# A gated convolution and mixture-of-experts layer on one Trainium2 core: small broadcast loads replaced by TensorE products, one load held back, one weight split moved two slots

## The chip, the cores and the metric

The kernel runs on one core of a Trainium2 chip. The metric is the device time of one execution in microseconds (us). Three executions of the kernel before gave 218.25, 219.16 and 421.25 us; their median is 219.16 us.

## The reference, cut to what matters

`x` and `ctx` are (16, 128, 256) in float32. The layer is

```python
x = x + tanh(g_xattn[0]) * xattn(ctx, ctx, layernorm(x), ssm_kernel, D)
x = x + tanh(g_ffn[0]) * ffn(layernorm(x), Wg, W1, W3, W2, sw1, sw3, sw2)
```

`xattn` splits the 128 channels into 16 heads of 8. For each head it forms the 8 x 8 products of the context with itself at every position, convolves each of them causally along the 256 positions with the head's filter `ssm_kernel[h]`, adds `D[h]` times the unconvolved product (the skip factor), multiplies with the normalised `x` and sums over one of the two channel indices. Adding `D[h]` to the filter's first tap gives the same result, since that tap multiplies the product at its own position.

`ffn` is a mixture of 8 experts (hidden size 352, top 1 of a softmax, 256 tokens of room per expert) plus one shared expert that sees every token: `silu(x W1) * (x W3) @ W2`, times the gate.

## The kernel before, in words

The work runs in *slots*, a loop over `s` that every engine writes out in its own program, and the engines meet at semaphores. The 16 batches form 4 groups of 4. Slots 0 to 31 hold the convolutions: slot `s` is group `s // 8` and two heads of it (a "unit"). From slot 16 on the shared expert is laid between them, and behind the slots come the 8 experts.

In slot `s`:

- TensorE convolves (`convolve`, L1078 to L1102): per head a 128 x 144 product (L1097) and a 128 x 288 product (L1100) of `kv` with `toep`, the filter's Toeplitz matrix, into PSUM tile `z[s % 2]`. It waits for the `kv` products, for the load of the two to four heads of `toep` that it needs, and from slot 2 on for VectorE to have emptied `z` of slot `s - 2` (`prods`, L1092).
- VectorE multiplies the result with the normalised `x` into `terms` (`products`, L860, six TENSOR_TENSOR instructions at L461).
- GpSimd (POOL in the profile) and ScalarE (ACT) form the `kv` products of the context for the next group (`kv_products` L442 and L445, `squares` L712), one quarter of a group in every second slot. The first quarter of group 0 is VectorE's.
- Layer norms are split: VectorE takes the statistics (L842 to L848), GpSimd the power -0.5 (`scale_and_bias`, L586 and L587), ScalarE applies them (L691). TensorE transposes the result (`turn_q` L1112) and ScalarE copies it to `qr` (`q_copy`). For group 0 that happens ahead of slot 0; `turn_q(1)` is in slot 5, `turn_q(2)` in slot 13.
- In slots 9 and 10 TensorE transposes and sums the terms of group 0 (`turn_r`, L1125, 32 matmuls each), and VectorE adds the result to `x_sb`, scaled by `tg`, the tanh of the gates (`first_residual`, L876, in slots 10 and 11). The second layer norm of group 0 follows: statistics in slot 11, scale in slot 12, apply on ScalarE in slot 13 (`norm2`), and `turn_xT` on TensorE in slot 14 (L1137).

The start. SyncE (SP) issues, in this order: two halves of `x` of group 0, `d_bc` (two skip factors, read with a step of zero so that every partition gets them, L529), the Toeplitz rows of heads 0 and 1 straight from the raw filter (L530), and then, after it has waited for `skip_added`, the store of the corrected filter to DRAM (`kskip`, L533), `x` of group 1 (L534), and, after the store has landed, the Toeplitz loads of heads 2 to 3, 4 to 7, then the context of group 1, then heads 8 to 11 and 12 to 15 (L500). The two gates (L541 and L542), again read with a step of zero to every partition, the router's weights, the shared expert's weights and the later groups follow. ScalarE issues `kp` (the filter), `dcol` (16 skip factors), the first quarter of the context of group 0 (L783) and the rest of it (L784). VectorE adds `dcol` to the filter's tap in `kp` (L1009), which raises `skip_added`, and later adds the skip factor to the diagonal of the Toeplitz matrices of heads 0 and 1, which came from the raw filter (L1021), reading `d_bc`.

TensorE fills its time up to `turn_q(0)` with 50 transposes of the identity that nobody reads (`TURNS`, L1230).

The shared expert's matmuls run in a high and a low part of the weights. ScalarE rounds the weights (`weights_high(0)`, L771, in slot `SPLIT_HIGH` = 11), then VectorE and GpSimd subtract, each for its half (`weights_low(0)` L986 and `split_up` L627, in slot `SPLIT_SLOT` = 12). The first user is slot 16. ScalarE computes `tg` and puts the router's weights in place in slot `ROUTER_SLOT` = 4 (L793 and L795).

Of the kernel before, what the change touches and what calls it, by code (L numbers as in the profile page):

```python
# [32 lines left out]
ALU = mybir.AluOpType  # L33
ACT = mybir.ActivationFunctionType
AX_X = mybir.AxisListType.X

P = 128
B, CH, L = 16, 128, 256
DH = 8
H = CH // DH  # L40
# [22 lines left out]
OUT_OF_RANGE = 4096.0  # L63
SPLIT_HIGH, SPLIT_SLOT = 11, 12
SETS = 5
SGS = 3
ROUTER_SLOT = 4
KVQ = 4 * KVH
KVRING = 5
REST_SLOT = 21  # L70
TERMS = 8
TURNS = 50
FULL_TERMS = 2
# [128 lines left out]
def build(nc, x, ctxt, kpad, skip_d, g_x, g_f, wg, w1, w3, w2, sw1, sw3, sw2, out):  # L202
# [4 lines left out]
    with ExitStack() as ctx:  # L207
        def sb(name, shape, dt=F32):
            return ctx.enter_context(nc.sbuf_tensor(name, shape, dt))

        def sem(name):
            return ctx.enter_context(nc.semaphore(name))
# [33 lines left out]
        ident = sb("ident", [P, P])  # L246
        anti = sb("anti", [P, P])
        d_bc = sb("d_bc", [P, 2])
        kp = sb("kp", [H, KPAD])
        tri = sb("tri", [P, P])  # L250
        ones = sb("ones", [P, P])
        dcol = sb("dcol", [H, 1])
        gates = sb("gates", [P, 2])
        tg = sb("tg", [P, 2])
# [47 lines left out]
        toep_first = sem("toep_first")  # L302
        d_in = sem("d_in")
        anti_turned = sem("anti_turned")
        diag_added = sem("diag_added")
# [172 lines left out]
        def _(sp):  # L478
# [49 lines left out]
            load_x(0)  # L528
            sp.dma_start(d_bc[:, :], bass.AP(skip_d.tensor, skip_d.offset, [[0, P], [1, 2]])).then_inc(d_in, 16)  # L529
            sp.dma_start(toep[:, 0:2, :],  # L530
# [9 lines left out]
            load_toeplitz(3)  # L540
            sp.dma_start(gates[:, 0:1], bass.AP(g_x.tensor, g_x.offset, [[0, P], [1, 1]])).then_inc(small_in, 16)  # L541
            sp.dma_start(gates[:, 1:2], bass.AP(g_f.tensor, g_f.offset, [[0, P], [1, 1]])).then_inc(small_in, 16)  # L542
            sp.dma_start(wg_sb[:, :, :], wg.rearrange("(k p) e -> p k e", p=P)).then_inc(small_in, 16)
# [141 lines left out]
        def _(act):  # L685
# [96 lines left out]
            act.dma_start(dcol[:, :], bass.AP(skip_d.tensor, skip_d.offset, [[1, H], [1, 1]])).then_inc(skip_in, 16)  # L782
            act.dma_start(ct[:, 0, 0:4 * CW], ctxt[0, :, 0:4 * CW]).then_inc(ctx_first, 16)  # L783
            act.dma_start(ct[:, 0, 4 * CW:], ctxt[0, :, 4 * CW:]).then_inc(ctx_in[0], 16)  # L784
            norm1(0)
            for c in range(1, 4):
# [3 lines left out]
            for s in range(SLOTS):  # L790
                if s == ROUTER_SLOT:
                    act.wait_ge(small_in, 16 * 3)
                    act.activation(tg[:, :], gates[:, :], ACT.Tanh).then_inc(tanh_done, 1)  # L793
                    act.wait_ge(dve_consts, 6)
                    act.activation(pads[:, 0:2, 0:E], wg_sb[:, :, :], ACT.Copy).then_inc(router_placed, 1)  # L795
# [31 lines left out]
        def _(dve):  # L827
# [180 lines left out]
            dve.wait_ge(skip_in, 32)  # L1008
            dve.tensor_tensor(kp[:, P - 1:P], kp[:, P - 1:P], dcol[:, :], ALU.add).then_inc(skip_added, 1)  # L1009
            norm_stats(0)  # L1010
            dve.wait_ge(ctx_first, 16)
# [5 lines left out]
            dve.wait_ge(anti_turned, 1)  # L1017
            dve.wait_ge(d_in, 16)
            dve.wait_ge(toep_first, 16)
# [57 lines left out]
        def _(pe):  # L1077
# [150 lines left out]
            pe.transpose(fb[0][:, 0:P], anti[:, :], ident[:, :]).then_inc(anti_turned, 1)  # L1228
            for _ in range(TURNS):
                pe.transpose(tp[1][:, 0:P], ident[:, :], ident[:, :])  # L1230
            turn_q(0)
            convolve(0)
            for s in range(SLOTS):
                if 1 <= s < CONV:
                    convolve(s)
                if s in SHARED_AT:
                    feed_forward(FU_AT[SHARED_AT[s]])
# [46 lines left out]
```

## Time and profile before

| what | value |
|---|---|
| median of three executions | 219.16 us |
| the profiled execution, its own time | 219.47 us |
| its span, first to last instruction | 217.7 us |
| TensorE busy | 201.6 us, 93% of the span |
| VectorE busy | 148.4 us, 68% |
| GpSimd busy | 125.1 us, 57% |
| ScalarE busy | 80.7 us, 37% |
| mean granted clock of TensorE | 0.993 of full speed |

The profile names engines PE (TensorE), PEld (its weight loads, which overlap), DVE (VectorE), ACT (ScalarE), POOL (GpSimd) and SP (SyncE); a q behind the name is the engine's instruction queue, as where it issues a DMA. L1097 is line 1097 of the kernel. An instruction's idle time is shown in brackets with what ended it. The profiled execution took 1.8 us more than its span.

### The profile page before, as it was taken

The numbers are of one execution on the slowest core, as the hardware profiler recorded it, in microseconds if no ns is written. First come the engines' busy times: TensorE is split into PE (matmuls) and PEld (weight loads), VectorE is DVE, ScalarE is ACT, GpSimd is POOL, SyncE is SP. The second block draws the span as 40 slices with busy tenths as digits, with TensorE's granted clock in tenths as the row PEclk, the third lists the DMA queues.
The fourth block names the chain that finished last, engine by engine and source line by source line (L and its number), as shares of the span: only waits on it lengthen the run. The fifth ranks groups of instructions, "written<-read, shape, count | busy, mean of one in ns | idle before, by whom it ended". The sixth has DMA issues, their size and how long they took to land.

```text
span 217.7 us, 4054 instructions
## 1 busy us (share of the span) xinstructions
PE 201.6 (93%) x1395; PEld 184.6 (85%) x1395; DVE 148.4 (68%) x488; ACT 80.7 (37%) x152; POOL 125.1 (57%) x129
## 2 busy tenths in 40 slices
PE   5978999969999999999999998999999999999970
PEld 5856789758998989898989998999999999999950
DVE  4678898699788987589867847353755775567230
ACT  2334412471653551322336237223354245423200
POOL 4399937486854599614682270540085587775751
PEclk9999999999999999999999999999999999999997
DMA  3789995000000010010201899833537669422221
GB/s 111 280 212 350 368 402 231 0 0 2 6 0 0 3 49 17 34 50 0 97 3 49 280 357 354 296 88 94 168 98 236 228 224 312 133 62 92 71 67 48
DMA packets 21926, 29.77 MB, mean 137 GB/s; under 512 B 3263, under 2 KB 19399, under 8 KB 21905
## 3 DMA queue, kind: packets, MB, share of 16 engines
q1 hardware_dynamic: 19248, 22.65, 31.7%
q0 software_dynamic: 2304, 6.05, 8.4%
q10 hardware_dynamic: 352, 0.81, 1.2%
q8 instruction: 11, 0.18, 0.4%
q14 instruction: 11, 0.08, 0.1%
HBM read 21.32 MB, written 8.45 MB: 137 GB/s over the span
## 4 chain that ended last, share of the span: by engine, by line
PE 76%; POOL 6%; DVE 4%; DMA 4%; issue 4%; ACT 2%; POOLq 1%; ACTq 1%; DVEq 0%
PE fb L1188 16%; PE z L1188 13%; PE z L1212 12%; PE tp L1125 10%; PE z L1100 9%; PE fb L1212 6%; PE z L1097 5%; POOL kv L442 4%; DMA ct<-ctxt 4%; DVE terms L461 2%; PE tp L1223 2%; POOL kv L445 1%; PE tp L1137 1%; DVE wl_gu L986 1%; ACT xrow L691 1%
## 5 line engine op out<-in xcount | busy, mean ns | idle before, releaser
L461 DVE TENSOR_TENSOR terms<-z,qr 128x512 f32<-128x512 f32 (+2 forms) x192 | 48.9, 326 | 7.3 <-PE z L1100 7.2
L1100 PE MATMUL z<-kv,toep 128*128 128x288 f32 x128 | 41.5, 406 | 0.0
L442 POOL TENSOR_TENSOR kv<-ct 128x768 f32<-128x768 f32 x15 | 28.3, 1884 | 13.9 <-PE z L1100 8.3
L668 POOL DMA_INDIRECT kv<-out,tok x16 | 22.3, 1392 | 18.2 <-DMA out<-x_sb 13.6
L1188 PE MATMUL fb<-xTh,wh_gu 128*128 128x256 f32 (+1 forms) x104 | 32.3, 311 | 0.2 <-issue 0.2
L1097 PEld LDWEIGHTS z<-kv,toep 128*128 128x128 f32 x128 | 22.2, 190 | 10.9 <-issue 7.0
L1097 PE MATMUL z<-kv,toep 128*128 128x144 f32 x128 | 26.8, 291 | 4.1 <-DMA toep<-kskip_scratch 2.3
L1188 PE MATMUL fb<-xTl,wh_gu 128*128 128x256 f32 (+1 forms) x104 | 29.0, 279 | 0.0
L1188 PE MATMUL fb<-xTh,wl_gu 128*128 128x256 f32 (+1 forms) x104 | 29.0, 279 | 0.0
L614 POOL TENSOR_TENSOR terms<-terms 128x512 f32<-128x512 f32 x16 | 20.3, 1286 | 11.1 <-DVE terms L461 11.1
L619 POOL DMA_INDIRECT xd_scratch<-xrow,dest x16 | 16.1, 1003 | 17.4 <-DVE xrow L921 7.3
L1188 PE MATMUL z<-xTh,wh_gu 128*128 128x256 f32 (+1 forms) x88 | 25.7, 292 | 0.0
L1188 PE MATMUL z<-xTl,wh_gu 128*128 128x256 f32 (+1 forms) x88 | 24.4, 278 | 0.0
L1188 PE MATMUL z<-xTh,wl_gu 128*128 128x256 f32 (+1 forms) x88 | 24.4, 277 | 0.0
L679 POOL DMA_INDIRECT out<-kv,tok x16 | 16.1, 1007 | 12.8 <-DVE kv L962 8.2
L1125 PE MATMUL tp<-ident,terms 128*128 128x128 f32 x192 | 23.0, 277 | 0.0
L1125 PEld LDWEIGHTS tp<-ident,terms 128*128 128x128 f32 x192 | 22.2, 193 | 0.3
L758 ACT ACTIVATE sg<-fb 128x256 f32<-128x256 f32 (+1 forms) x26 | 9.8, 376 | 31.4 <-PE fb L1188 29.5
L1188 PEld LDWEIGHTS fb<-xTh,wh_gu 128*128 128x128 f32 (+1 forms) x104 | 19.3, 186 | 1.3 <-issue 0.6
L1100 PEld LDWEIGHTS z<-kv,toep 128*128 128x128 f32 x128 | 20.0, 190 | 0.0
L1188 PEld LDWEIGHTS fb<-xTh,wl_gu 128*128 128x128 f32 (+1 forms) x104 | 19.3, 186 | 0.7
L1188 PEld LDWEIGHTS fb<-xTl,wh_gu 128*128 128x128 f32 (+1 forms) x104 | 19.3, 185 | 0.0
(132 smaller groups left out, 389.5 us busy)
## 6 DMA issues: line engine op xcount, KB each, us to landing
terms<-w SPq DMA_DIRECT2D x16, 352.0 KB, 8.3
ct<-ctxt SPq DMA_DIRECT2D x3, 768.0 KB, 8.5
xd_scratch<-xrow SPq DMA_DIRECT2D x4, 516.0 KB, 9.9
kv<-xd_scratch SPq DMA_DIRECT2D x8, 258.0 KB, 5.1
out<-x_sb SPq DMA_DIRECT2D x8, 256.0 KB
terms<-w SPq DMA_DIRECT2D x8, 256.0 KB, 8.3
x_sb<-x SPq DMA_DIRECT2D x3, 512.0 KB, 6.5
toep<-kskip_scratch SPq DMA_DIRECT2D x3, 512.0 KB, 8.0
```

The source lines that it names most:

```text
L442: eng.tensor_tensor(dst, left, right, ALU.mult)
L461: return eng.tensor_tensor(view(terms, t0 + row * TROW + col, [[64, 2], *td]), view(src, zo, [[512, 2], *zd]), view(qr, q0 + qo, [[CW, 2], ...
L614: pool.tensor_tensor(low, low, high, ALU.add).then_inc(folded, 1)
L619: pool.indirect_dma_start(out=xd, out_offset=bass.IndirectOffsetOnAxis(ap=dest[:, n:n + 1], axis=0), in_=xrow[:, g % 2, b, :], in_offset=N ...
L668: pool.indirect_dma_start(out=bg[:, e % BRING, t, :], out_offset=None, in_=out_rows, in_offset=bass.IndirectOffsetOnAxis(ap=tok[:, e, t:t ...
L679: pool.indirect_dma_start(out=out_rows, out_offset=bass.IndirectOffsetOnAxis(ap=tok[:, e, t:t + 1], axis=0), in_=fin[:, e % 2, t, :], in_o ...
L758: act.activation(sg[0:n, k % SGS, :], bank[0:n, 0:256], ACT.Silu).then_inc(silu_done, 1)
L1097: pe.matmul(view(z[s % 2], k * 512 + GB, [[PL, NPL], [1, GB]]), toep[:, h, P:2 * P], view(kv, o, [[PL, NPL], [1, GB]]), start=True, stop=F ...
L1100: mm = pe.matmul(z[s % 2][:, k, 0:KVH], toep[:, h, 0:P], view(kv, o, [[1, KVH]]), start=False, stop=True, skip_group_check=True)
L1125: mm = pe.matmul(tp[n % 2][:, j * P:(j + 1) * P], src, ident[:, :], is_transpose=True, start=(t == 0), stop=(t == terms_of(g) - 1))
L1188: mm = pe.matmul(bank[0:rows(blk, c), m * 256:(m + 1) * 256], wt[w % 2][:, col:col + rows(blk, c)], xt[:, place, k, first:first + 256], st ...
L1212: mm = pe.matmul(bank[:, t * L:(t + 1) * L], hidden(blk, c)[0:rows(blk, c), t * P:(t + 1) * P], down[0:rows(blk, c), c * L:(c + 1) * L], s ...
```

## The change

Seven edits, which belong to three things.

1. The skip factors of heads 0 and 1 no longer come by the DMA to 128 partitions. VectorE multiplies two columns of the identity with `dcol` (`d_of`, 16 x 2), TensorE multiplies that with a 16 x 128 block of ones into PSUM (`fb[1]`), and ScalarE copies it to `d_bc`. The idle transposes are now 22 ahead of that product and 22 behind it. The gates come as one element each to one partition; TensorE spreads them in slot 6, where it waits for `small_in`, and ScalarE takes the tanh from PSUM. `ROUTER_SLOT` goes from 4 to 6.
2. ScalarE waits for `skip_added` before it issues the rest of the context of group 0. SyncE's store of the filter waits for the same semaphore, as before.
3. The split of the shared weights goes from slots 11 and 12 to slots 9 and 10.

```diff
-SPLIT_HIGH, SPLIT_SLOT = 11, 12
+SPLIT_HIGH, SPLIT_SLOT = 9, 10
-ROUTER_SLOT = 4
+ROUTER_SLOT = 6
-TURNS = 50
+TURNS = 22
+        d_of = sb("d_of", [H, 2])
-        gates = sb("gates", [P, 2])
+        gates = sb("gates", [1, 2])
...
             load_x(0)
-            sp.dma_start(d_bc[:, :], bass.AP(skip_d.tensor, skip_d.offset, [[0, P], [1, 2]])).then_inc(d_in, 16)
...
-            sp.dma_start(gates[:, 0:1], bass.AP(g_x.tensor, g_x.offset, [[0, P], [1, 1]])).then_inc(small_in, 16)
-            sp.dma_start(gates[:, 1:2], bass.AP(g_f.tensor, g_f.offset, [[0, P], [1, 1]])).then_inc(small_in, 16)
+            sp.dma_start(gates[:, 0:1], bass.AP(g_x.tensor, g_x.offset, [[0, 1], [1, 1]])).then_inc(small_in, 16)
+            sp.dma_start(gates[:, 1:2], bass.AP(g_f.tensor, g_f.offset, [[0, 1], [1, 1]])).then_inc(small_in, 16)
...
             act.dma_start(ct[:, 0, 0:4 * CW], ctxt[0, :, 0:4 * CW]).then_inc(ctx_first, 16)
+            act.wait_ge(skip_added, 1)
             act.dma_start(ct[:, 0, 4 * CW:], ctxt[0, :, 4 * CW:]).then_inc(ctx_in[0], 16)
+            act.wait_ge(spread, 1)
+            act.activation(d_bc[:, :], fb[1][:, 0:2], ACT.Copy).then_inc(d_in, 1)
             norm1(0)
...
                 if s == ROUTER_SLOT:
                     act.wait_ge(small_in, 16 * 3)
-                    act.activation(tg[:, :], gates[:, :], ACT.Tanh).then_inc(tanh_done, 1)
+                    act.wait_ge(spread, 2)
+                    act.activation(tg[:, :], fb[1][:, 2:4], ACT.Tanh).then_inc(tanh_done, 1)
...
             dve.tensor_tensor(kp[:, P - 1:P], kp[:, P - 1:P], dcol[:, :], ALU.add).then_inc(skip_added, 1)
+            dve.wait_ge(pool_consts, 1)
+            dve.tensor_scalar(d_of[:, :], ident[0:H, 0:2], dcol[:, 0:1], None, ALU.mult).then_inc(d_chosen, 1)
             norm_stats(0)
...
-            dve.wait_ge(d_in, 16)
+            dve.wait_ge(d_in, 1)
...
-            for _ in range(TURNS):
-                pe.transpose(tp[1][:, 0:P], ident[:, :], ident[:, :])
+            def turns(n):
+                for _ in range(n):
+                    pe.transpose(tp[1][:, 0:P], ident[:, :], ident[:, :])
+
+            turns(TURNS)
+            pe.wait_ge(dve_consts, 2)
+            pe.wait_ge(d_chosen, 1)
+            pe.matmul(fb[1][:, 0:2], ones[0:H, :], d_of[:, :], start=True, stop=True).then_inc(spread, 1)
+            turns(TURNS)
             turn_q(0)
             convolve(0)
             for s in range(SLOTS):
                 if 1 <= s < CONV:
                     convolve(s)
+                if s == ROUTER_SLOT:
+                    pe.wait_ge(small_in, 16 * 3)
+                    pe.matmul(fb[1][:, 2:4], ones[0:1, :], gates[:, :], start=True, stop=True).then_inc(spread, 1)
```

## Rows read from the trace of the kernel before

**Rows 1.** The page, busy us of TensorE, share of the span, instructions

```profile
PE 201.6 (93%) x1395; PEld 184.6 (85%) x1395; DVE 148.4 (68%) x488; ACT 80.7 (37%) x152; POOL 125.1 (57%) x129
```

**Rows 2.** Windows by stage: length, busy us by engine, PEclk, DMA share, GB/s

```profile
42.00:50.40 8.40, 6.02 (x36) 4.67 (x36) 8.33 (x28) 5.08 (x10) 6.93 (x7) 1.00 0.00 0
50.40:110.00 59.60, 59.16 (x413) 53.96 (x412) 48.95 (x193) 23.16 (x44) 36.53 (x36) 1.00 0.07 23
```

**Rows 3.** Waits of TensorE, 10 to 30 and 30 to 212 us: total, times, longest

```profile
PE z L1097 <- DMA toep<-kskip_scratch: 2.3, 3, 1.6
...
PE z L1097 <- DVE terms L461: 1.5, 3, 0.9
```

**Rows 4.** The chain that ended last, 0 to 35 us: start, length, what

```profile
2.31 7.78 DMA ct<-ctxt
...
27.42 0.48 PE z L1097 x2
```

**Rows 5.** Timeline, the DMA issues of SyncE and ScalarE at the start

```profile
1.81 0.46 SPq L529 DMA_DIRECT2D d_bc<-skip_d  x1
...
2.31 0.47 ACTq L784 DMA_DIRECT2D ct<-ctxt  x1
...
4.60 0.35 SPq L533 DMA_DIRECT2D kskip_scratch<-kp  x1
...
10.53 0.88 SPq L500 DMA_DIRECT2D toep<-kskip_scratch  x2
```

**Rows 6.** DMA issues, the last figure is us from issue to landing

```profile
toep<-kskip_scratch SPq DMA_DIRECT2D x1, 256.0 KB, 3.9
...
kp<-kpad ACTq DMA_DIRECT2D x1, 23.9 KB, 2.4
kskip_scratch<-kp SPq DMA_DIRECT2D x1, 23.9 KB, 5.9
```

**Rows 7.** Windows of half a us, columns as in rows 2

```profile
3.00:3.50 0.50, 0.50 (x4) 0.50 (x3) 0.00 (x0) 0.50 (x1) 0.30 (x1) 1.00 1.08 369
...
4.50:5.00 0.50, 0.50 (x4) 0.50 (x3) 0.50 (x3) 0.00 (x0) 0.00 (x0) 1.00 0.02 6
...
11.00:11.50 0.50, 0.50 (x7) 0.50 (x6) 0.06 (x1) 0.47 (x2) 0.50 (x1) 1.00 0.06 20
...
13.50:14.00 0.50, 0.00 (x0) 0.00 (x0) 0.47 (x3) 0.00 (x0) 0.50 (x1) 1.00 0.94 287
```

**Rows 8.** Timeline, 0 to 34 us: the work up to the end of slot 7

```profile
2.45 7.59 PE L1230 MATMUL tp<-ident 128*128 128x128 f32 x50
...
10.16 1.90 POOL L442 TENSOR_TENSOR kv<-ct 128x768 f32<-128x768 f32 x1 [2.11 <-DMA ct<-ctxt]
...
11.77 1.41 DVE L842 BATCH_NORM_STATS2 stats<-x_sb 128x6 f32<-128x256 f32 x4 [0.71 <-DMA x_sb<-x]
...
14.25 1.53 DVE L461 TENSOR_TENSOR terms<-z,qr 128x512 f32<-128x512 f32 x6
...
18.12 2.07 ACT L691 ACTIVATE xn<-x_sb,nbias,rstd 128x256 f32<-128x256 f32 x4 [5.20 <-POOL nbias L587]
...
20.20 0.48 PE L1097 MATMUL z<-kv,toep 128*128 128x144 f32 x2 [0.38 <-DMA toep<-kskip_scratch]
...
22.10 0.20 ACT L793 ACTIVATE tg<-gates 128x2 f32<-128x2 f32 x1 [1.29 <-DMA wg_sb<-wg]
...
23.19 1.04 PE L1112 MATMUL tp<-ident,xn 128*128 128x128 f32 x8
...
25.73 3.01 DVE L461 TENSOR_TENSOR terms<-z,qr 128x512 f32<-128x512 f32 x12 [0.79 <-PE z L1100]
```

**Rows 9.** Timeline, 33 to 60 us: around the weight split

```profile
39.23 0.75 DVE L876 SCALAR_TENSOR_TENSOR x_sb<-tp,tg,x_sb 128x512 f32<-128x512 f32 x1 [1.98 <-PE tp L1125]
...
45.67 2.59 DVE L986 TENSOR_TENSOR wl_gu<-shared_gu,wh_gu 128x768 fp32r<-128x768 f32 x1
...
48.45 1.09 PE L1137 MATMUL tp<-ident,xrow 128*128 128x128 f32 x8 [0.85 <-ACT xrow L691]
```

More of the change, by code:

```diff
@@ L303, in build @@
         d_in = sem("d_in")
+        d_chosen = sem("d_chosen")
+        spread = sem("spread")
         anti_turned = sem("anti_turned")
```

## The prediction

> **What bounds the kernel now.** I read the page first: TensorE is busy for 201.6 of 217.7 us [rows 1]. The windows by stage say where it isn't. From 50.4 to 110 us it works 59.16 of 59.60 us, while 42.0 to 50.4 us has 6.02 of 8.40 [rows 2]; the remaining holes lie ahead of 28 us and behind the last matmul. So a microsecond that the start saves is kept if TensorE reaches the end of slot 7 earlier and finds its inputs there, and elsewhere only the 2.4 us of holes around 45 us are to be had.
>
> The waits of TensorE name the start's limit: 2.3 us in three waits for the Toeplitz loads, and from 30 us on 1.5 us in three waits for VectorE to empty `z` [rows 3]. The chain of waits tells another story, and the reader must correct it. It runs back from the matmul at 27.42 over GpSimd's `kv` products to the context load that was issued at 2.31 and took 7.78 us [rows 4]. But that matmul is slot 8, whose wait asks for four `kv` products (L1085), and GpSimd had then finished seven. What ended its wait is `prods`: VectorE's products of slot 6 end at 25.73 + 3.01/2 = 27.24 [rows 8]. So the path is: filter's store, its landing, Toeplitz loads, convolution of slots 1, 2, 4, and VectorE behind them. VectorE's products of slots 0 to 7 run from 14.25 to 28.74 [rows 8], 14.5 us for eight times 1.51 = 12.1 us of work; 2.4 us are waits for TensorE. TensorE's slot 9 needs slot 7's products, and from there it is the bound.
>
> The timeline of the queues shows why the loads are late: the store is issued at 4.60, lands 5.9 us later, and the first load follows at 10.53 [rows 5, 6]. `kp`, of the same 23.9 KB, took 2.4 us [rows 6]. Ahead of the store in its own ring are `x`, `d_bc` and a Toeplitz load, beside it the whole context.
>
> **The change part by part.** *The broadcast load.* `d_bc` is issued at 1.81 [rows 5]. The DMA engines move 369 GB/s at 3.0 us and 6 GB/s at 4.5 to 5.0, with a DMA share of 0.02, though a Toeplitz load and 768 KB of context are queued [rows 7]. I take this hole, about 1.3 us, to be the 128 reads of 8 bytes from one address, which stand just there in the order. If they are not its cause, it stays: gain between 0 and 1.3 us of DMA time.
>
> *The held-back context.* The 576 KB rest is issued at about 4.65, not 2.31 [rows 5]. The store then has ahead of it `x` (524 kB), the Toeplitz load (262), the context's first quarter (197) and `kp` (24): 1007 kB, at 369 GB/s [rows 7] 2.7 us from about 2.2, so the engines are clear at 5 us. The store's landing is bounded by the two rows of [rows 6]: 4.60 + 2.4 = 7.0 and 4.60 + 5.9 = 10.5. I take 7.4, near the low end, for nothing bulky is left in front of it and only the rest of the context and `x` of group 1 run beside it.
>
> The first Toeplitz load goes out at 7.4 and not 10.53: 3.1 us earlier. It took 3.9 us [rows 6], so it lands at 11.3, not 14.4. The following ones keep their spacing if the engines have no more to move than before; the hole at 11.0 to 11.5 (20 GB/s [rows 7]), in which SyncE's wait left them empty, is filled by `x` of group 1. Slot 4's matmuls began at 20.20, when their load had landed [rows 8]; now at 17.1. Slot 2's load lies between, at about 13.5.
>
> `x` of group 1 landed at 11.77 [rows 8]. Now 1007 + 24 + 590 + 524 kB are to be moved up to it, with the last 1138 kB from about 5.9: 9.0 to 9.4 us.
>
> *VectorE and the eight slots.* Before, its first `kv` quarter, half of group 0's norm and the diagonals ran from 8.3, when the context's first quarter landed, to 11.06 [rows 7]; then it waited for `x` until 11.77, and the statistics of group 1 took 2.5 us up to 14.25 [rows 8]. Now the first quarter is there by 6, the statistics of group 0 end at 6.7, and 2.8 + 2.5 us later it is 12.0. The products of slot 0 start there and not at 14.25, now behind `q_copy`, too. Slot 1's follow at 13.5, slot 2's at 15.2 (slot 2's matmuls need slot 0's products), slot 3's at 16.7, slot 4's at 18.5 (17.1 and 1.4 us of matmuls), slot 5's at 20.0, slot 6's at 22.5 behind `turn_q(1)` (1.04 us [rows 8]), slot 7's at 24.2. They end at 25.7 against 28.74: 3.0 us earlier. The floor for this is a start at 11.6 with no wait but `turn_q`: 24.3, a gain of 4.4; the other end is a start held to the old order, 0.
>
> *GpSimd.* It started at 10.16, when the context's rest landed, and ScalarE's norm of group 1 ended 10.0 us later, at 18.12 + 2.07 [rows 8]. `turn_q(1)` is now due at 19.9, so the rest of the context may land up to about 9.8 without harm. Its 590 kB beside `x` from 5.9 on give 8.5 to 9.2. This is the thinnest cover in the sum: each us past 9.8 costs one.
>
> *The spread.* The 50 transposes took 7.59 us, 0.152 each [rows 8]. Twenty-two end at 5.8, when `d_of` (VectorE at 4.75, one small instruction ahead of the statistics) is there; the product and its PSUM copy on ScalarE, idle until 8.1, give `d_bc` by 6.7; 22 more end near 9.4, where `xn` ends. Cost 0 to 0.4; I take 0, since VectorE's statistics and not `turn_q(0)` start slot 0. The gates' product adds some 0.2 us to TensorE in slot 6, I take 0.1 on the path. Its wait for `small_in` lets everything behind it in TensorE's order wait, the convolution of slot 7 first. The loads landed at 22.1 [rows 8] and slot 6's matmuls end at 22.4 in my sum: even unshifted the loads are in time, so 0. ScalarE waits for that product, but what it has behind it, a quarter's square, is needed eight slots later.
>
> *The split.* VectorE's part takes 2.59 us at 45.67 [rows 9] and stood ahead of the products of slot 13, for which TensorE waited 0.32 us at 49.86. In slot 10 it comes before the residual that VectorE waited 1.98 us for, at 39.23 [rows 9]; ending 0.6 us late it is still ahead of the next matmuls' end. ScalarE's part goes into a stretch in which it waits for GpSimd. Of the 2.4 us of holes only that one goes: the 0.88 us wait stands behind the statistics of slot 11, and the 0.85 us at 48.45 [rows 9] behind ScalarE's norm, both untouched. Gain 0.3; bounds 0 and, should half of the holes go, 1.2.
>
> **Sum.** 3.0 - 0.1 + 0.3 = 3.2 us off the profiled execution: 219.47 gives 216.3. The median of the runs is 0.3 us lower: 219.16 gives 216.0. That is 1.5%; about 2% either way (214.8 and 223.5 us) is what a measurement of this kernel tells from no change.
>
> The Trainium skill ("DMA: Bandwidth & Descriptors", Queues, rings and completion order) says that each DMA engine goes round robin between the rings of SyncE and ScalarE, a packet at a time. By that rule the old context load took only turns beside the store, and most of the store's 5.9 us came from its own ring; holding the load back would be worth about half of my figure, and the total some 217.5. No row separates the two rings; I keep the sum because `d_bc` leaves the store's own ring as well.
>
> **The rivals.**
>
> A. *More than 2%.* The store lands at 7.0, slot 0's products start at 11.6 and the DMA engines run without a hole: 4.4 us, and the split frees 0.3 to 1.2. Time 213.9 to 214.6. For it: `kp`'s 2.4 us. Against: while the Toeplitz loads ran the engines moved 287 GB/s and not 369 [rows 7], so slot 4 still waits.
>
> B. *The held-back load eats the gain.* The 590 kB land late, GpSimd starts late, and `turn_q(1)` waits. At 12.4 (7.8 us from its issue as before [rows 4]) it costs 2.6 us and leaves 0.6: 218.6. Past 13.0 us the kernel is slower than before; at 13.5 it is 219.7. For it: GpSimd has next to no idle time there. Against: the DMA hole that stretched the 7.8 us would be gone.
>
> C. *The store is no earlier*, because the hole is a matter of the start and not of `d_bc`, and what queues ahead is the Toeplitz load: landing at 9.5, gain 1: 218.2.
>
> D. *The clock.* Six idle transposes fewer and a wait between them. At half the clock a slot's matmuls take 3.0 us and not about VectorE's 1.5, `turn_q` 2.1: TensorE needs 8 x 3.0 + 2 x 2.1 = 28 us from 9.4 and ends slot 7 at 37.6, 8.9 later than now: 228. Against: the granted clock is 1.00 in a half us in which TensorE did nothing [rows 7]. The Trainium skill ("TensorE: Matmul & The Clock Gate", Part 1) lets the clock fall from 2.4 to 1.2 GHz when the engine is idle; the rows show the full clock through the waits of the start.
>
> **How the numbers follow.** Forecast 0.57 (215.0 to 217.4), A 0.22, B 0.10, C 0.08, D 0.03. A lies below 214.8, D above 223.5, B mostly within. So faster by over 2%: 0.22 and a little of the forecast's own tail, 0.24; slower: 0.03; same: 0.73. The range, with the end of A and the middle of B and C, goes from 213.9 to 218.7.
>
> **What would show it.** Right: no `d_bc` issue, no half us near 4.5 with an idle DMA; the store lands near 7.4 and the next Toeplitz load is issued there; slot 0's products start near 12, slot 8's matmuls near 24.3 and slot 9's near 25.7; the split at about 34 with no wait of TensorE for `z` at 49.9 less the shift. From there the gap to the old trace stays at 3.2 us to the end. Wrong: the store still takes over 4 us (C), `turn_q(1)` waits for ScalarE (B), TensorE waits for `small_in` in slot 6, a clock below 1.00 ahead of the end (D), or a gap that closes again behind slot 16.

## The result, and the profile after

The changed kernel is slightly slower: 219.58 us (median of 14 runs) against 218.69, ratio 1.005 with a 95% interval of 1.0029 to 1.0071. The prediction said 216.0 with a range of 213.9 to 218.7; it is wrong in size and in sign. Two runs of the kernel before, one here (421.25 us) and one beside the experiments (432.11 us), took about twice as long, for a reason that no profile shows; they do not move the medians. The profiled execution took 219.54 us with a span of 217.8, which is an ordinary one for this kernel, while the one of before (219.47 us, span 217.7) lay 0.8 us above its own median. The two traces therefore look equal where the medians are not.

The timeline of the changed kernel at the start, to be held against [rows 5] and [rows 8]:

```profile
4.30 0.35 SPq L535 DMA_DIRECT2D kskip_scratch<-kp  x1
4.31 0.37 ACTq L787 DMA_DIRECT2D ct<-ctxt  x1
...
4.70 0.43 SPq L496 DMA_DIRECT2D x_sb<-x  x1
...
6.58 1.90 POOL L588 TENSOR_TENSOR rstd<-veps,mhalf 128x4 f32<-128x4 f32 x1 [3.28 <-DVE mneg L854]
...
8.04 0.91 SPq L503 DMA_DIRECT2D toep<-kskip_scratch  x2
...
11.20 1.81 POOL L445 TENSOR_TENSOR kv<-ct 128x768 f32<-128x768 f32 x1 [2.44 <-DMA ct<-ctxt]
...
12.09 1.06 ACT L723 ACTIVATE qr<-tp 128x512 f32<-128x512 f32 x2
...
12.26 1.41 DVE L848 BATCH_NORM_STATS2 stats<-x_sb 128x6 f32<-128x256 f32 x4 [2.20 <-DMA x_sb<-x]
...
13.39 1.80 POOL L445 TENSOR_TENSOR kv<-ct 128x768 f32<-128x768 f32 x1
...
14.11 1.10 DVE L853 TENSOR_SCALAR veps<-mv 128x4 f32<-128x4 f32 x1
...
15.20 2.99 DVE L464 TENSOR_TENSOR terms<-z,qr 128x512 f32<-128x512 f32 x12
...
16.88 0.48 PE L1105 MATMUL z<-kv,toep 128*128 128x144 f32 x2 [1.44 <-DVE terms L464]
...
25.73 0.38 PE L1253 MATMUL fb<-gates,ones 1*128 1x2 f32 x2
```

The reader sees the intended part happen and be paid for at once. The filter's store lands at 8.04 and not at 10.53. But the context's rest lands at 11.2 instead of 10.1, `x` of group 1 at 12.26 instead of 11.77, `q_copy(0)`, which ScalarE does behind its squares of that context, starts at 12.09 instead of 11.18, and VectorE's products of slot 0 start at 15.20, 0.95 us later than before. TensorE has nothing to do from 15.44 to 16.88.

The later `x` alone would explain only half of these 0.95 us. The other half is one small instruction at the end of VectorE's statistics, which computes `veps` (L853 here, L847 before). It lasts until GpSimd's `kv` product beside it ends: 14.11 + 1.10 = 15.21 against 13.39 + 1.80 = 15.19. In the trace of before it is the same:

```profile
12.42 1.81 POOL L442 TENSOR_TENSOR kv<-ct 128x768 f32<-128x768 f32 x1
...
13.62 0.64 DVE L847 TENSOR_SCALAR veps<-mv 128x4 f32<-128x4 f32 x1
```

The two ends, 14.26 and 14.23, again lie 0.03 us apart. In all fifteen profiles of this case with the statistics of group 1 ahead of slot 0, this instruction ends 0.02 to 0.04 us behind a `kv` product of GpSimd, and slot 0's products start 0 to 0.4 us later. GpSimd starts its first `kv` product when the context's rest lands, 1.04 us later than before. So it was the held-back load itself, by way of GpSimd, that ended last, and not `x`.

The DMA issues of the start, with us to landing (before, in this order: 7.8, 6.7, 3.9 and 5.9):

```profile
ct<-ctxt ACTq DMA_DIRECT2D x1, 576.0 KB, 6.8
...
x_sb<-x SPq DMA_DIRECT2D x1, 512.0 KB, 7.5
...
toep<-kskip_scratch SPq DMA_DIRECT2D x1, 256.0 KB, 5.6
...
kskip_scratch<-kp SPq DMA_DIRECT2D x1, 23.9 KB, 3.7
```

The store gained 2.2 us, the Toeplitz load behind it lost 1.7 and `x` 0.8.

The waits of TensorE from 10 to 30 us. Before, [rows 3] had 2.3 us for the Toeplitz loads, and the same view named no wait for VectorE:

```profile
PE z L1105 <- DVE terms L464: 2.0, 3, 1.4
PE z L1105 <- DMA toep<-kskip_scratch: 1.2, 1, 1.2
```

One wait took the place of the other. The weight split went as foreseen; VectorE's part took 0.96 us instead of 2.59 [rows 9], for GpSimd's half no longer ran all the way beside it, and the wait before slot 15 is gone:

```profile
37.78 0.96 DVE L992 TENSOR_TENSOR wl_gu<-shared_gu,wh_gu 128x768 fp32r<-128x768 f32 x1
```

The matmuls of slot 9's sum (`turn_r`) are a good place to take the balance. They start at 30.42 before and at 31.04 after, and to the end of the span it is 187.3 us before and 186.8 after. So between these two profiles the start lost 0.6 us and the split gave 0.5 back.

One thing no single profile shows. The mean granted clock of the fourteen runs of the changed kernel is 0.989 to 0.996 in ten of them, median 219.5 us, and 0.982 to 0.985 in four, which took 220.9 to 221.9 us. Of 140 runs of the kernel before that were made beside the experiments, one lies below 0.988. The profiled run of the changed kernel is not one of the four (0.991), so no trace shows where its clock falls.

### The profile page after: what moved, and what is told of

It reads as the page before. It is cut to its first block, busy times and chain, and to the rows that moved or that the text cites. A ratio compares the mean times of both kernels' runs of the same rounds, so it can differ in the third digit from the quotient of the medians.

```text
span 217.8 us, 4053 instructions
## 1 busy us (share of the span) xinstructions
PE 201.3 (92%) x1393; PEld 183.8 (84%) x1393; DVE 146.9 (67%) x489; ACT 80.7 (37%) x153; POOL 125.1 (57%) x129
## 3 DMA queue, kind: packets, MB, share of 16 engines
HBM read 21.32 MB, written 8.45 MB: 137 GB/s over the span
## 4 chain that ended last, share of the span: by engine, by line
PE 81%; DMA 5%; ACT 4%; DVE 4%; issue 3%; POOLq 1%; ACTq 0%; SPq 0%; DVEq 0%; POOL 0%
PE fb L1196 15%; PE z L1196 13%; PE z L1220 12%; PE z L1108 11%; PE tp L1133 10%; PE z L1105 6%; PE fb L1220 6%; DMA x_sb<-x 3%; DVE terms L464 2%; ACT xrow L693 2%; PE tp L1145 2%; PE tp L1231 2%; DMA dcol<-skip_d 1%; ACT qr L723 1%; PE tp L1120 1%
## 5 line engine op out<-in xcount | busy, mean ns | idle before, releaser
L445 POOL TENSOR_TENSOR kv<-ct 128x768 f32<-128x768 f32 x15 | 27.3, 1822 | 13.1 <-PE z L1108 9.5
L670 POOL DMA_INDIRECT kv<-out,tok x16 | 22.3, 1392 | 18.2 <-DMA out<-x_sb 13.7
```

The lines of the kernel that those rows point to most:

```text
L445: eng.tensor_tensor(dst, left, right, ALU.mult)
L670: pool.indirect_dma_start(out=bg[:, e % BRING, t, :], out_offset=None, in_=out_rows, in_offset=bass.IndirectOffsetOnAxis(ap=tok[:, e, t:t ...
```

## The experiments

All have twelve runs each, in four groups in the order of the table, each beside 35 runs of the kernel before on the same chip: its median was 218.81 us for the first four kernels, 218.88 for the next four, 218.94 for the third four and 219.16 for the last. The ratio is estimated for itself and is not the quotient of the two medians. "Low" counts the runs with a mean clock of 0.987 or less. "Store" and "sum" are, in each profile, when the first Toeplitz load behind the filter's store was issued and when slot 9's sum of terms began.

| kernel | us | ratio (95%) | low | store | slot 0's products | sum | sum to end |
|---|---|---|---|---|---|---|---|
| before | 218.69 | | | 10.53 | 14.25 | 30.42 | 187.3 |
| changed | 219.58 | 1.005 (1.0029 to 1.0071) | 4 of 14 | 8.04 | 15.20 | 31.04 | 186.8 |
| e0_same | 219.14 | 1.0004 (0.9979 to 1.0029) | 0 | 9.42 | 13.40 | 29.41 | 187.4 |
| e1_split | 218.42 | 0.9988 (0.9965 to 1.0011) | 0 | 10.77 | 14.53 | 30.95 | 186.7 |
| e2_hold | 219.82 | 1.0047 (1.0017 to 1.0076) | 4 | 8.45 | 15.27 | 32.15 | 187.5 |
| e3_spread | 219.39 | 1.0033 (1.0005 to 1.0061) | 1 | 9.84 | 13.91 | 30.28 | 187.3 |
| e4_nohold | 219.24 | 1.0037 (1.0013 to 1.0061) | 2 | 9.71 | 13.72 | 30.18 | 186.9 |
| e5_skip | 219.19 | 1.0018 (1.0001 to 1.0036) | 0 | 9.99 | 14.06 | 30.01 | 187.5 |
| e6_after_order | 219.02 | 1.0009 (0.9986 to 1.0032) | 2 | 7.41 | 15.85 | 33.17 | 186.8 |
| e7_split_order | 219.17 | 1.0009 (0.9990 to 1.0029) | 0 | 10.49 | 13.08 | 30.92 | 186.7 |
| e8_turns30 | 219.08 | 1.0012 (0.9987 to 1.0037) | 1 | 8.90 | 14.57 | 30.40 | 186.7 |
| e9_warm | 219.63 | 1.0028 (1.0010 to 1.0046) | 0 | 9.31 | 15.71 | 31.55 | 186.8 |
| e10_split_hold_order | 218.59 | 0.9981 (0.9962 to 1.0001) | 0 | 8.27 | 12.75 | 30.68 | 186.8 |
| e11_split_quarters | 218.32 | 0.9977 (0.9957 to 0.9997) | 1 | 10.42 | 14.28 | 30.41 | 187.0 |
| e12_split_hold_x | 218.35 | 0.9969 (0.9947 to 0.9991) | 0 | 10.15 | 13.32 | 29.83 | 186.8 |
| e13_after_gates | 219.11 | 0.9993 (0.9960 to 1.0025) | 5 | 8.34 | 14.85 | 30.18 | 186.7 |
| e14_after_x | 219.06 | 0.9995 (0.9978 to 1.0012) | 0 | 10.37 | 13.53 | 31.03 | 186.9 |
| e15_split_x | 220.41 | 1.0052 (1.0019 to 1.0084) | 5 | 12.16 | 14.55 | 32.93 | 186.8 |

The last column is the first lesson: with the old split 187.3 to 187.5, with the new one 186.7 to 187.0, whatever was done to the start. What the first 30 us lose or gain is kept to the end, as the prediction said, and the split is worth 0.6 us there (0.3 to 0.8 from kernel to kernel).

### The parts, one at a time

> The kernel before, unchanged, as its own control. Both theories: 219 us, ratio 1.000. It shows which mean clocks the old kernel has in its runs; by theory C (too few idle transposes) none of them lies at 0.985 or below, as four of the changed kernel's did.

A ratio of 1.0004, no difference, as it should be, and no low clock. Its median is still 0.3 us above that of the runs beside it, so 0.3 us between medians is no more than their scatter. Its profile has the unchanged kernel's store landing 1.1 us earlier than the profile of before, and its slot 0 products 0.85 us earlier. The start of this kernel varies by about a us between runs of the same program; a difference of half a us between two single profiles means nothing there. That holds for the columns "store", "products" and "sum" of the table, too.

```diff
-SPLIT_HIGH, SPLIT_SLOT = 11, 12
+SPLIT_HIGH, SPLIT_SLOT = 9, 10
```

> Only the shared weights' split in slots 9 and 10. Theory M (each part has a price of its own, and they cancel): 0.5 us faster, 0.9975, because TensorE's slots 13 to 15 wait less; the start is unchanged, slot 0's products at 14.25 us. Theory C: the same gain and no run at a low clock, so the changed kernel's loss lies wholly elsewhere.

0.4 us below the kernel before by the medians; the interval includes no change. The trace is clearer, with 186.7 us from slot 9's sum to the end.

```diff
+            act.wait_ge(skip_added, 1)
             act.dma_start(ct[:, 0, 4 * CW:], ctxt[0, :, 4 * CW:]).then_inc(ctx_in[0], 16)
```

> Only ScalarE's wait for skip_added ahead of the context's rest. Theory M: the filter's store lands at about 9 us instead of 10.5, but the context's rest at 11 or later instead of 10.1, and x of group 1 after 12; ScalarE's squares and with them q_copy(0) and slot 0's products come about 1 us later: 0.5 to 1 us slower. Theory C: no effect on the clock; the store's earlier landing makes it up to 1 us faster.

1.0 us slower. The late arrivals of theory M are there: GpSimd starts on the context's rest at 10.91, `x` comes at 12.00, slot 0's products at 15.27. The low clock is there, too, though this kernel has all its 50 idle transposes, so theory C names the wrong cause. Its profile caught the fall. Windows of half a us of this kernel, columns as in [rows 2]:

```profile
4.50:5.00 0.50, 0.50 (x4) 0.50 (x3) 0.48 (x3) 0.00 (x0) 0.00 (x0) 1.00 0.80 223
...
6.50:7.00 0.50, 0.50 (x7) 0.50 (x6) 0.50 (x3) 0.00 (x0) 0.15 (x1) 1.00 0.34 65
16.00:16.50 0.50, 0.00 (x0) 0.00 (x0) 0.50 (x4) 0.00 (x0) 0.50 (x1) 1.00 1.03 369
17.00:17.50 0.50, 0.50 (x2) 0.50 (x3) 0.50 (x2) 0.00 (x0) 0.50 (x3) 0.50 1.10 377
20.50:21.00 0.50, 0.50 (x4) 0.42 (x3) 0.50 (x2) 0.50 (x2) 0.50 (x1) 1.00 1.17 379
```

and its timeline of TensorE at the same place:

```profile
16.95 0.82 PE L1098 MATMUL z<-kv,toep 128*128 128x144 f32 x2 [2.50 <-DVE terms L461]
17.56 1.17 PE L1101 MATMUL z<-kv,toep 128*128 128x288 f32 x2
```

TensorE stood idle for 2.5 us, waiting for slot 0's products; then the granted clock is 0.50, its lower level of 1.2 GHz, until about 20 us, and the pair of 288-column matmuls takes 1.17 us and not 0.65. The four low runs average 221.3 us, the eight others have a median of 219.4. So a low clock costs 1.8 us in one run of three, and the late arrivals 0.6 in all of them.

The third part is the whole change without hold and split: 44 idle transposes, skip factors and gates by TensorE.

> Only the skip factors and gates by TensorE (44 idle transposes, router slot 6); context not held, split in slots 11 and 12. Theory M: the hole in the DMA at 4.5 us goes, the context's rest lands before 9.5 us, slot 0's products start up to 1 us earlier, and the gates' product in slot 6 gives 0.4 us back: 0 to 0.6 us faster. Theory C: slower by 0.5 to 1 us, with a mean clock at or below 0.985 in about a third of the runs.

0.6 us slower, where 0 to 0.6 faster was expected. The DMA windows say why nothing was gained. e3_spread, which loads no `d_bc`, still has the hole:

```profile
4.00:4.50 0.50, 0.50 (x4) 0.50 (x3) 0.25 (x3) 0.13 (x1) 0.00 (x0) 1.00 0.92 128
4.50:5.00 0.50, 0.50 (x4) 0.50 (x3) 0.50 (x3) 0.00 (x0) 0.00 (x0) 1.00 1.31 65
5.00:5.50 0.50, 0.50 (x6) 0.50 (x5) 0.50 (x3) 0.00 (x0) 0.00 (x0) 1.00 0.71 96
```

while e2_hold, which has `d_bc`, moves 223 GB/s there and has its hole at 6.5 us with 65 GB/s. So the hole is not the broadcast load's in the main. In the kernels that leave `x` behind the store its emptiest half us begins 1.2 to 2.7 us behind the issue of the context's rest, at 2.3 without the hold and at 4.3 to 4.8 with it. A small part may be `d_bc`'s: in that half us the three kernels without it and without the hold (e3, e4, e5) move 65 to 87 GB/s, the five profiles with it and without the hold that leave `x` in its place 6 to 48.

### The parts in pairs, and what each was paid for

> The changed kernel without the hold: spread and split together. Theory S (from slot 0's products on everything follows rigidly, so the time is their start plus a constant): no mean clock below 0.988, slot 0's products at about 13.9 us as in the spread alone, 218.8 us. Rival (the parts do not add up): as slow as the changed kernel, 219.6, with low clocks.

219.24, with two low runs of twelve; the others have a median of 219.16. The split does not show on top of the spread in the medians (0.15 us, within their scatter) or in the ratios; it does in its last column. Theory S was 0.4 us too low here.

> Only the skip factors by TensorE (with 44 idle transposes); gates as before, no hold, no split. Theory S: the gates' product in slot 6 is what the spread alone paid for, 0.4 us; without it 218.9 us, the kernel before's time. Rival (the 8-byte broadcast load costs 1.3 us of DMA time, as the prediction had it): 218.0 or less.

219.19 and no low clock. The skip factors by TensorE bring nothing, with `d_bc` gone; they cost 0 to 0.8 us by the interval, and its trace does not show where: slot 9's sum begins at 30.01, within what e0_same and the kernel before span. Theory S in its number was 0.3 low, the rival (218.0) is out.

```diff
             norm1(0)
+            q_copy(0)
             for c in range(1, 4):
                 squares(0, c)
-            q_copy(0)
...
-            dve.wait_ge(x_in[1], 16)
-            norm_stats(1)
             for s in range(SLOTS):
+                if s == 1:
+                    dve.wait_ge(x_in[1], 16)
+                    dve.wait_ge(rstd_done, 1)
+                    for b in range(2):
+                        dve.bn_stats(stats[:, b, :], x_sb[:, GB + b, :])
+                if s == 2:
+                    norm_stats(1, 2)
```

> The changed kernel with two orders of work changed: ScalarE copies q of group 0 ahead of its squares, which wait for the held-back context, and VectorE takes the statistics of group 1 behind the products of slots 0 and 1, so that slot 0 waits for neither x of group 1 nor the context's rest. Theory S: slot 0's products start at 13 us instead of 15.2, the wait of TensorE before slot 2 goes, no low clock any more, 217.6 us. Rival (the Toeplitz loads or VectorE's total bound the slots anyway): 219.3, the low clocks gone or not.

> The kernel before with the split in slots 9 and 10 and the same two orders of work, without hold or spread. Theory S: slot 0's products at 13 us, but the Toeplitz load for slot 1 at 13.5 to 14.6 as before, so VectorE waits after slot 0; 217.8 us, no low clock. Rival: 218.4, as with the split alone.

e6 came to 219.02, near the rival's 219.3, and e7 to 219.17, slower than both 217.8 and 218.4. Theory S fell in e7: slot 0's products did start at 13.08, 1.2 us earlier, and slot 9's sum began no earlier (30.92). The 2.5 us of statistics are now between the products, VectorE takes turns with TensorE and has no slack to hide them in; against the split alone the order costs 0.5 us by the ratios, with intervals that overlap. The start of slot 0's products is a bound only if all that VectorE owes before slot 8 is counted with it. e6 took back 0.6 to 0.9 us of the changed kernel's loss where theory S gave it 2.0, and its profile shows another way into the low clock:

```profile
7.06 2.01 POOL L588 TENSOR_TENSOR rstd<-veps,mhalf 128x4 f32<-128x4 f32 x1 [3.75 <-DVE mneg L854]
...
9.39 2.37 DVE L1023 TENSOR_SCALAR xn<-x_sb,rstd,nbias 128x256 f32<-128x256 f32 x2 [0.98 <-POOL nbias L589]
...
11.91 1.06 PE L1125 MATMUL tp<-ident,xn 128*128 128x128 f32 x8 [2.26 <-DVE xn L1023]
```

with, later in the same profile,

```profile
13.50:14.50 1.00, 1.00 (x4) 0.71 (x4) 0.00 (x0) 0.97 (x3) 1.00 (x2) 0.50 0.97 386
```

GpSimd's power takes 2.0 us instead of 1.0, now that VectorE's first `kv` quarter runs beside it, and VectorE's half of the norm takes 2.37 us instead of 0.73 beside GpSimd's next product. The same two instructions in the kernel before:

```profile
6.76 1.01 POOL L586 TENSOR_TENSOR rstd<-veps,mhalf 128x4 f32<-128x4 f32 x1 [3.45 <-DVE mneg L848]
...
9.64 0.73 DVE L1015 TENSOR_SCALAR xn<-x_sb,rstd,nbias 128x256 f32<-128x256 f32 x2
```

In e6 the idle transposes had ended at 9.65, TensorE waits 2.26 us for `xn`, and the clock is at its lower level from 13 to 16 us, for slot 0 and the start of slot 1.

### The clock

```diff
             pe.matmul(fb[1][:, 0:2], ones[0:H, :], d_of[:, :], start=True, stop=True).then_inc(spread, 1)
-            turns(TURNS)
+            turns(TURNS + 8)
```

> The changed kernel with 8 idle transposes more behind the spread (22 and 30), so that TensorE is busy until about 10.6 us. Theory G1 (the clock falls in some runs because the shortened idle row ends at 9.4 us and xn comes up to 2 us later): no mean clock at or below 0.987, median 219.4. Theory G2 (it falls in the wait before slot 2): a third of the runs still at 0.982 to 0.986, median 219.6.

```diff
             for s in range(SLOTS):
+                if s == 2:
+                    for _ in range(12):
+                        pe.transpose(fb[0][:, 0:P], ident[:, :], ident[:, :])
```

> The same, and 12 more idle transposes into a free PSUM tile ahead of slot 2's matmuls, 1.8 us of them in the stretch in which TensorE waits for VectorE. If G1 or G2 or both hold, no mean clock at or below 0.987, and the slowest runs of 221 us go; median 219.4, still 0.6 above the kernel before, since the late start of slot 0's products stays.

With the longer idle row one run of twelve is low, with the filler ahead of slot 2 as well none is, and the slowest run is 220.1 us. Neither G1 (none) nor G2 (a third) is met. Twelve runs are few, 4 of 14 against 1 of 12 is no proof. The profiles of e2 and e6 show the fall behind an idle TensorE at either place; that the waits bring it also in the changed kernel is likely and not shown. e9's median, which stays at 219.63, says that the clock is only part of the loss. The filler does not pay: e9 is 0.4 us slower than e8 by the ratios, with intervals that overlap.

### Hold without spread, and the hole

> The kernel before with the split, the hold and the two orders of work, but with the skip factors and gates loaded as before and its 50 idle transposes. If the gates' product (0.4 us) and not the hold is what the changed kernel with the orders still loses: 218.4 us, slot 0's products near 13. Rival (with the hold VectorE and the Toeplitz loads come no earlier than without): 219.0.

218.59, 0.9981 with an interval up to 1.0001, no low run. Each against its own kernel before, it is 0.5 us below e6, with intervals that overlap; what it lacks is the spread. It is no better than the split alone.

```diff
-            act.dma_start(ct[:, 0, 4 * CW:], ctxt[0, :, 4 * CW:]).then_inc(ctx_in[0], 16)
+            for i in range(1, 4):
+                act.dma_start(ct[:, 0, 4 * i * CW:4 * (i + 1) * CW],
+                              ctxt[0, :, 4 * i * CW:4 * (i + 1) * CW]).then_inc(ctx_in[0], 16)
...
-            eng.wait_ge(ctx_in[g], 16)
+            eng.wait_ge(ctx_in[g], 16 if g else 48)
```

> The kernel before with the split, and the rest of the context loaded as three quarters with rows of 1536 bytes instead of one load with rows of 4608. Theory H1 (the hole in the DMA 1.7 us behind that load's issue comes from its long rows): no half us under 150 GB/s from 4 to 6 us, slot 0's products near 13, 217.5 us. H2 (it is the start of any further traffic on the second queue): the hole stays, 218.4 us as with the split alone.

H1 is out: with rows of 1536 bytes the hole is there, no shallower than in the split alone (48 GB/s at its lowest), and the store lands as late.

```profile
4.50:5.00 0.50, 0.50 (x4) 0.50 (x3) 0.50 (x2) 0.50 (x1) 0.00 (x0) 1.00 0.45 58
5.00:5.50 0.50, 0.50 (x5) 0.50 (x4) 0.50 (x3) 0.08 (x1) 0.00 (x0) 1.00 0.31 44
```

### The failed step moved, and the gates' product undone

```diff
-            sp.wait_ge(skip_added, 1)
-            sp.dma_start(kskip, kp[:, :]).then_inc(skip_stored, 16)
             load_x(1)
+            sp.wait_ge(skip_added, 1)
+            sp.dma_start(kskip, kp[:, :]).then_inc(skip_stored, 16)
```

e12 has this with the split, the hold and the q copy first; e14 is the changed kernel with this and the q copy first; e15 is the split with this alone.

> The kernel before with the split, the hold, ScalarE's q copy ahead of its squares, and x of group 1 issued ahead of the filter's store instead of behind it. Theory X (the hold lost because x of group 1, behind the context's long rows, landed at 12.3 and set slot 0's products): x lands by 9 us, slot 0's products start near 12.5, the store lands at 8.5 to 9, slot 9's sum of terms starts near 28.7 instead of 29.7, 217.3 us. Rival Y (what x gains the store or the Toeplitz loads lose): 218.4.

> The changed kernel with x of group 1 ahead of the filter's store and the q copy ahead of the squares. Theory X: slot 0's products near 12.5, 217.9 us, no low clock since the wait before slot 2 goes. Rival Y: 219.3.

> The kernel before with the split and x of group 1 ahead of the store, without the hold. Theory X: without the hold the store is then behind x, too, lands at 11.5 instead of 10, and the Toeplitz loads come late: 219.3 us, slower than the split alone. This shows what the hold is good for once x is out of its way; if instead it is 218.4, the order of the two does not matter.

In e12 the timeline shows `x` there at 10.0 or before, and slot 0's products at 13.32:

```profile
10.00 1.40 DVE L843 BATCH_NORM_STATS2 stats<-x_sb 128x6 f32<-128x256 f32 x4
...
11.50 1.81 POOL L442 TENSOR_TENSOR kv<-ct 128x768 f32<-128x768 f32 x1 [2.84 <-DMA ct<-ctxt]
...
11.85 1.49 DVE L848 TENSOR_SCALAR veps<-mv 128x4 f32<-128x4 f32 x1
...
13.32 1.53 DVE L461 TENSOR_TENSOR terms<-z,qr 128x512 f32<-128x512 f32 x6
...
13.96 0.48 PE L1098 MATMUL z<-kv,toep 128*128 128x144 f32 x2 [1.44 <-DMA toep<-kskip_scratch]
```

Theory X is right that an early `x` brings slot 0's products forward, and Y in the time (218.4 expected). `x` comes 2.3 us earlier than in the changed kernel and the products 1.9. The lines show how: the last small instruction of the statistics comes at 11.85 and so lasts until the end of GpSimd's first `kv` product (11.50 + 1.81 = 13.31) and not of its second. e14 shows the same. But the store is behind `x` in the same queue and lands at 10.15, as if nothing had been held. What is left is 218.35 us, 0.9969 (0.9947 to 0.9991): the lowest ratio of all kernels here, 0.3% under the kernel before and clearly under the changed one; from e1, e10 and e11 its interval does not set it apart. e14, the changed kernel with the same move, comes to 219.06 with no low run, nearer to Y (219.3) than to X (217.9). e15 shows what the hold is good for once `x` is ahead (its other difference from e12, the place of the q copy, is in no queue of the DMA): without it the store lands at 12.16, TensorE waits 2.78 us for slot 1's load, and five of twelve runs are low. Where 219.3 us was expected, 220.41 came; the seven other runs have a median of 219.7. The wait and the stretched pair behind it:

```profile
16.14 0.48 PE L1097 MATMUL z<-kv,toep 128*128 128x144 f32 x2 [2.78 <-DMA toep<-kskip_scratch]
16.46 1.02 PE L1100 MATMUL z<-kv,toep 128*128 128x288 f32 x2
```

e13 is the changed kernel with the gates loaded and the tanh taken as before.

> The changed kernel with the gates loaded to all partitions as before and tanh in slot 4; no product in slot 6. If that product costs the 0.4 us that the traces show between slots 6 and 7: 219.1 us, slot 9's sum of terms 0.4 us closer to slot 0's products; low clocks in some runs as in the changed kernel. Rival (the two broadcast loads cost the DMA engines as much): 219.6.

219.11, as foreseen, but against a kernel before at 219.16. From slot 0's products to slot 9's sum it is 15.33 us here and 15.84 in the changed kernel, so the product costs 0.5 us of TensorE's path. The pair e3 and e5, which differ in it alone, has 16.37 and 15.95, 0.4 us. By the ratios it is 0.3 us in that pair, but 1.2 us between e13 and the changed kernel (0.9993 against 1.005, each with its interval, so 0.4 to 2.1). Five of e13's twelve runs are low; the seven others have a median of 218.6, 0.5 us under the kernel before, which is better than the parts of the account below allow. The changed kernel was not run again beside the experiments, so part of its loss may lie in that one comparison.

## Why the prediction was wrong

**What bounds the kernel** was read rightly in the main. From slot 1 to slot 8 the chain's GpSimd piece was not the path (ahead of slot 0 it was, as said below); the slots up to 8 go by VectorE's products; and what the first 30 us save or lose arrives at the end, in every kernel of the table.

**The broadcast load** was given the hole in the DMA, "which stand just there in the order". That step failed. The order fitted a second candidate as well, the context's rest, issued half a us later; e3_spread and e5_skip take `d_bc` away and keep the hole, shallower at most by a little, e2_hold keeps `d_bc` and moves the hole. Rival C named this, with 0.08.

**The held-back context.** The store's landing was said at 7.4 and came at 8.04 in the profile, at 7.41 to 9.31 in the six other kernels that hold the context and leave `x` behind the store. The Toeplitz load behind it was said to take its old 3.9 us and took 5.6, since it now shares the engines with what was held back. The term that broke the sum is the next one: "`x` of group 1 [...] 9.0 to 9.4 us" measured 12.26, and the context's rest, "8.5 to 9.2", measured 11.2. The sum divided the bytes by 369 GB/s, the rate of one full half us (the kernel before holds 366 for 3 us, from 6.5 to 9.5), and left the hole out, since it believed it had been removed with `d_bc`. The hole came back 2 us later, in front of just these two loads: 136 GB/s in the changed kernel where 342 had been moved 1.5 us earlier. From 8.04 us on, moreover, the two share the engines with the Toeplitz loads, whose earlier issue was the aim of the change, and from 8.99 on with the context of group 1; the sum gave these bytes no share. From 5.0 to 12.0 us the engines moved 266 GB/s.

```profile
4.50:5.00 0.50, 0.50 (x4) 0.50 (x3) 0.50 (x2) 0.29 (x1) 0.00 (x0) 1.00 0.99 342
...
6.00:6.50 0.50, 0.50 (x6) 0.33 (x4) 0.47 (x6) 0.00 (x0) 0.00 (x0) 1.00 0.63 136
```

**VectorE and the eight slots.** A start of slot 0's products at 12.0 was said, it was 15.20. Two things came together: the statistics waited for `x` until 12.26, and their last small instruction then lasted until the end of GpSimd's second `kv` product, which follows the context's rest by 4.0 us. The statistics were put at 2.5 us as in the trace of before, where 0.5 us of that already was this stretching; here they took 2.9. No term of the sum led from the context's rest to slot 0 by way of GpSimd. A third term was missing, though it did not end last here: ScalarE's squares stand ahead of `q_copy(0)` in its program and wait for the context that the change holds back, so that `qr` is complete at 13.8 us and slot 0's products could not have begun at 12.0 in any case. e12 moves `x` and the q copy and gets 13.3. From there the slots went as said, with 14.1 us from the first products to the end of slot 7's against 13.7.

**GpSimd.** The cover was called the thinnest in the sum, with `turn_q(1)` due at 19.9. The context did come 1.4 us past the 9.8 that the sum allowed (rival B), but the slots themselves came later still, and ScalarE's norm ended 2 us ahead of `turn_q(1)`. The rival was the right place to look and not the way in which it cost: the late context cost by way of slot 0's start.

**The spread.** The skip factors were put at 0; 0.3 us slower is measured for them alone, with an interval that reaches down to 0. The gates' product was put at 0.1 us on the path; the traces show 0.4 between slots 6 and 7 and 0.4 to 0.5 from slot 0 to slot 9. TensorE is the pacemaker there, and its product of two columns runs 0.38 us with nothing beside it. No wait for `small_in` appeared.

**The split** was put at 0.3 with bounds of 0 and 1.2; it is 0.6 in the traces, and 0.4 in the medians, with an interval that includes no change.

**The clock** was rival D, with 0.03, argued away by one half us without work at full clock [rows 7]. It is neither as rare nor as dear as that: about a third of the runs of the changed kernel and of e2, 1.8 us each. What was wrong is the reading: that the clock stayed up behind the waits of one trace said nothing of the longer ones that the change might make. The Trainium skill ("TensorE: Matmul & The Clock Gate", Part 1) has the clock fall behind an idle engine. The rows of e2_hold, e6_after_order and e15_split_x agree, each with a wait of 2.3 to 2.8 us ahead of a granted clock of 0.50.

The account, in us: split -0.6, gates' product +0.5, hold +0.6 through the late arrivals and on average +0.5 through the clock (4 runs of 14 at 1.8), skip factors 0 to +0.3. That is +1.0 to +1.3. It has to be held against the means, since the clock's term is an average over the runs: 219.95 us against 218.77, without the run of 421.25, is +1.2. The medians give +0.9. Each term has a scatter of some 0.3 us, and e13 does not fit (above), so the sum shows that the terms can account for the loss and no more.

One figure of the prediction does not follow from its terms: 4.4 + 1.2 - 0.1 us take rival A, and with it the range, down to 213.7 and not 213.9. Nothing hangs on it.

What stays open: what the hole is. It follows the first large transfer behind the opening loads, on either queue (e12 has it at 4.5 us, 50 GB/s, and e14 from 4.0 us, 68 GB/s, with the context held and `x` issued early), with long rows or short. Only that it moves is shown. Open, too, are where the clock falls in the changed kernel's own low runs, and why the same program falls in some runs only.

## What to carry to other kernels

When a transfer is held back to let another one through, price the held one and everything behind it first, with the rate of the whole stretch and not of one full half us, with the share of what the earlier transfer lets loose, and list by program order what each engine does behind its wait. A dip in a resource goes to whatever follows it in time only if a second candidate has been ruled out; taking each away alone costs two runs. And where TensorE waits, ask whether a change lengthens one wait by a us: in these profiles waits of up to 1.7 us left the granted clock at 1.00, and in the three in which it fell to 0.50 a wait of 2.3 to 2.8 us stood ahead of it, at a cost of nearly 2 us more.

## What had not been expected

- The granted clock can fall in the middle of a kernel that is 93% busy on TensorE. In e2_hold it is 0.50 from about 16.7 to 20 us behind 2.5 us of idleness. By their mean clocks one run in three of that program has it; the others, at 0.988 to 0.994, have not.
- VectorE and GpSimd stretch each other: the power on GpSimd 1.01 to 2.01 us, VectorE's half norm 0.73 to 2.37, its part of the weight split 0.96 to 2.59, each by what ran beside it. A VectorE instruction of 128 x 4 elements that takes 0.17 us when GpSimd is idle took 0.64 to 1.49 in the fifteen profiles, up to the end of GpSimd's product. An earlier landing that lets two such instructions meet can cost more than it brings.
- The same program's first 10 us differ by a us from run to run: the store landed at 9.42 and at 10.53 in two profiles of the same kernel.

```profile
9.42 0.88 SPq L500 DMA_DIRECT2D toep<-kskip_scratch  x2
```

This is e0_same's timeline, to be held against the 10.53 of [rows 5].
